# Storing and loading the bfloat16 parts of q and k one by one

## The reference

```python
def _L0_xattn_ref(query, key, value, Wq, bq, Wk, bk, Wv, bv, Wo, bo):
    q = proj(query, Wq, bq)          # B, H=16, S=256, D_K=16
    k = proj(key, Wk, bk)
    v = proj(value, Wv, bv)
    q = q * cos + _rotate_half(q) * sin
    k = k * cos + _rotate_half(k) * sin
    scores = jnp.einsum('bhqd,bhkd->bhqk', q, k) / np.sqrt(D_K)
    scores = jnp.where(dist <= WINDOW, scores, -1e9)     # WINDOW = 50
    p = jax.nn.softmax(scores, axis=-1)
    out = jnp.einsum('bhqk,bhkd->bhqd', p, v)
    return out @ Wo.T + bo
x = x + jnp.tanh(g_xattn[0]) * _L0_xattn_ref(_layernorm(x), ctx_1024, ctx_1024, ...)
x = x + jnp.tanh(g_ffn[0]) * _L0_ffn_ref(_layernorm(x), L0_ffn_w_gate, L0_ffn_w_up, L0_ffn_w_down)
```

## Time and profile before

| what | value |
|---|---|
| median of three runs | 1368.07 us (1368.03 to 1373.25) |
| the profiled execution: its own time | 1368.83 us |
| its span, first to last instruction | 1367.1 us |
| mean granted TensorE clock | 0.965 |
| TensorE busy (matmul) | 1203.8 us, 88% |
| VectorE busy | 1212.9 us, 89% |
| ScalarE busy | 826.5 us, 60% |
| GpSimd busy | 549.5 us, 40% |
| moved by DMA | 207.27 MB, mean 152 GB/s |

### The profile page before, as it was taken

How to read it: one execution, slowest core, us unless ns; L and a number is a source line. 1 busy time by engine, 2 the same in 40 slices (tenths; PEclk the granted TensorE clock), 3 DMA queues, 4 the chain that set the end, 5 groups by cost and what they waited for, 6 DMA issues and landing times. The chain is left out here.

```text
span 1367.1 us, 27802 instructions
## 1 busy us (share of the span) xinstructions
PE 1203.8 (88%) x8963; PEld 786.5 (58%) x8995; DVE 1212.9 (89%) x3603; ACT 826.5 (60%) x1336; POOL 549.5 (40%) x1357
## 2 busy tenths in 40 slices
PE   5689898989998988998988659998999799968998
PEld 3457666666666666666666434443433334427887
DVE  3799999999999999999998849997999989988886
ACT  2255656666666665656565536665677599983332
POOL 1177777777777777777776610000000000000000
PEclk9699999999999999999999869999999999988999
DMA  2757575757565666666664202223455455546764
GB/s 78 156 121 183 135 174 139 168 139 164 143 161 146 158 151 153 154 151 158 146 161 112 102 8 93 111 97 127 158 183 185 159 191 196 199 165 205 241 225 169
DMA packets 132369, 207.27 MB, mean 152 GB/s; under 512 B 11159, under 2 KB 97050, under 8 KB 126106
## 3 DMA queue, kind: packets, MB, share of 16 engines
q1 hardware_dynamic: 132250, 205.86, 54.4%
HBM read 125.60 MB, written 79.69 MB: 150 GB/s over the span
## 5 line engine op out<-in xcount | busy, mean ns | idle before, releaser
L670 DVE CUSTOM_DVE_ANT_0 psum<-psum,band 128x178 f32<-128x178 f32 x1024 | 316.5, 372 | 38.4 <-PE psum L878 38.1
L552 ACT ACTIVATE probs<-psum 128x356 f32<-128x356 f32 x512 | 210.6, 468 | 162.7 <-PE psum L895 162.2
L486 POOL TENSOR_SCALAR_AFFINE_SELECT probs<-probs 128x154 f32<-128x154 f32 (+1 forms) x512 | 221.4, 443 | 156.5 <-ACT probs L552 150.5
L1088 PE MATMUL psum<-xnT,w_upT 128*128 (+1 forms) x1152 | 261.1, 384 | 19.0 <-DVE maxima L1312 8.8
L1088 PEld LDWEIGHTS psum<-xnT,w_upT 128*128 128x128 f16 x1152 | 109.9, 99 | 170.0 <-issue 32.6
L878 PE MATMUL psum<-k_stack,q_stack 96*128 96x178 bf16 x1024 | 141.3, 245 | 51.3 <-DVE smax L670 47.4
L495 POOL TENSOR_SCALAR_AFFINE_SELECT probs<-probs 128x254 f32<-128x254 f32 (+1 forms) x512 | 180.3, 375 | 0.0
L895 PE MATMUL psum<-q_stack,k_stack 98*128 98x178 bf16 x1024 | 136.2, 242 | 16.8 <-DMA q_stack<-shiftT 10.5
L670 DVE DVE_READ_ACCUMULATOR2_ANT smax<- 128x1 f32 x1024 | 142.9, 140 | 0.0
L1688 PE MATMUL psum<-w_downT,xnT 128*128 128x256 f16 x1152 | 128.3, 275 | 16.0 <-DVE xnT L1638 16.0
L878 PEld LDWEIGHTS psum<-k_stack,q_stack 96*128 96x128 bf16 x1024 | 74.2, 98 | 109.0 <-DVE smax L670 87.2
(11 more groups left out here) (189 smaller groups left out, 2265.3 us busy)
## 6 DMA issues: line engine op xcount, KB each, us to landing
k_parts_scratch<-k_parts SPq DMA_DIRECT2D x32, 384.0 KB, 2.5
q_parts_scratch<-q_parts SPq DMA_DIRECT2D x32, 384.0 KB, 2.6
k_stack<-k_parts_scratch SPq DMA_DIRECT2D x32, 384.0 KB, 5.1
q_stack<-q_parts_scratch SPq DMA_DIRECT2D x32, 384.0 KB, 7.3
gate_scratch<-g_stage SPq DMA_DIRECT2D x16, 768.0 KB, 3.2
g_in<-gate_scratch SPq DMA_DIRECT2D x16, 768.0 KB, 4.6
sig_scratch<-w_gateT SPq DMA_DIRECT2D x32, 384.0 KB, 2.3
sig_again<-sig_scratch SPq DMA_DIRECT2D x32, 384.0 KB, 3.4
```

The costliest lines, as they stand in the source:

```text
L486: nc.gpsimd.affine_select(out=t[:, :, 0:n], in_=t[:, :, 0:n], pattern=[[0, 2], [1, n]], compare_op=ALU.is_ge, fill=0.0, base=WINDOW - off, ...
L552: nc.scalar.activation(ring_tile(probs, b, pair, c)[:].rearrange("p e j -> p (e j)"), scoreT_bank[c][:, 0:2 * SPAN], ACT.Exp, scale=DK ** ...
L670: ins = nc.vector.tensor_tensor_reduce(out=mine, in0=mine, in1=keep["band"][:, t, :], scale=1.0, scalar=-3e38, op0=ALU.add, op1=ALU.max, a ...
L1088: last = nc.tensor.matmul(bank[:], weights[wp][:, c * I + f * P:c * I + (f + 1) * P], x_parts[:, c, bass.ds(j * (2 * TILE) + xp * TILE, TI ...
```

## The change

Each part gets its own store, of 128 KB, and is loaded as soon as the stores it waits for have landed. For k, a part goes to all row blocks that hold it, with one DMA each: three for the high part, two for the middle one, one for the low one, each of 16 rows of 8 KB (128 KB) that lie 3, 2 or 1 partitions apart. For q, a part is one DMA, as before: 384, 256 and 128 KB. So a batch has 6 stores and 9 loads where it had 2 and 6. Two semaphores per tensor take the place of one: `high_stored` for part 0, `rest_stored` for parts 1 and 2 together. The loads of parts 1 and 2 wait until both are stored. ScalarE's `high` waits for both semaphores. The store of k's high part stands ahead of the second half of b2's shift rows.

```diff
-            def store_parts(b, n):
+            def store_part(b, n, part):
                 if not b.real:
                     return
-                reached(sp, mid_ready[n], b, 1, 1)
-                reached(sp, low_ready[n], b, 1, 1)
+                reached(sp, part_ready[n][part], b, 1, 1)
                 if b.n >= NBUF:
-                    sp.wait_ge(stack_loaded[n][b.buf], b.rnd * 48)
-                sp.dma_start(scratch[n][b.buf].rearrange("k (a d) (h t) -> (d h) (k a) t", a=2, h=H),
-                             parts[n][:].rearrange("p k (a t) -> p (k a) t", a=2)).then_inc(parts_stored[n], 16)
+                    sp.wait_ge(stack_loaded[n][b.buf], b.rnd * LOADED[n])
+                sp.dma_start(scratch[n][b.buf, part].rearrange("(a d) (h t) -> (d h) a t", a=2, h=H),
+                             parts[n][:, part, :].rearrange("p (a t) -> p a t", a=2)).then_inc((rest_stored if part else high_stored)[n], 16)
-            def load_stacks(b, n):
+            def load_part(b, n, part):
...
-                reached(sp, parts_stored[n], b, 16, 16)
-                reached(sp, scoredT, b.before(NBUF), 2 * PAIRS, 2 * PAIRS)
+                if part:
+                    reached(sp, rest_stored[n], b, 32, 32)
+                else:
+                    reached(sp, high_stored[n], b, 16, 16)
+                    reached(sp, scoredT, b.before(NBUF), 2 * PAIRS, 2 * PAIRS)
                 row = 0
                 for g in range(3):
                     rows = (3 - g) * DK
-                    sp.dma_start(stack[row:row + rows, :, :].rearrange("r s t -> r (s t)"), scratch[n + "_rows"](b.buf, g)).then_inc(stack_loaded[n][b.buf], 16)
+                    if n == "q" and g == part:
+                        sp.dma_start(stack[row:row + rows, :, :].rearrange("r s t -> r (s t)"),
+                                     scratch[n][b.buf, part].unsqueeze(1).to_broadcast([DK, 3 - g, H * S]))\
+                            .then_inc(stack_loaded[n][b.buf], 16)
+                    if n == "k" and part < 3 - g:
+                        sp.dma_start(stack[row + part:row + rows:3 - g, :, :].rearrange("r s t -> r (s t)"),
+                                     scratch[n][b.buf, part]).then_inc(stack_loaded[n][b.buf], 16)
                     row += rows
...
                 load_residual(Batch(rnd, unit, 3))
+                store_part(Batch(rnd, unit, 0), "k", 0)
                 load_shift(Batch(rnd, unit, 2), 1)
-                store_parts(Batch(rnd, unit, 0), "k")
-                store_parts(Batch(rnd, unit, 0), "q")
-                load_stacks(Batch(rnd, unit, 0), "k")
-                load_stacks(Batch(rnd, unit, 0), "q")
+                b0 = Batch(rnd, unit, 0)
+                store_part(b0, "k", 1)
+                load_part(b0, "k", 0)
+                store_part(b0, "k", 2)
+                store_part(b0, "q", 0)
+                load_part(b0, "k", 1)
+                load_part(b0, "k", 2)
+                load_part(b0, "q", 0)
+                store_part(b0, "q", 1)
+                store_part(b0, "q", 2)
+                load_part(b0, "q", 1)
+                load_part(b0, "q", 2)
                 load_shift(Batch(rnd, unit, 1), 0)
...
-                reached(act, parts_stored[n], b.before(1), 16, 16)
+                reached(act, high_stored[n], b.before(1), 16, 16)
+                reached(act, rest_stored[n], b.before(1), 32, 32)
```

More of the change, by code:

```diff
@@ L277, in attention @@
         xres_loaded = [sem(f"xres_loaded{k}") for k in range(NBUF)]
-        parts_stored = {n: sem(f"{n}_parts_stored") for n in "qk"}
+        high_stored, rest_stored = ({n: sem(f"{n}_{size}_stored") for n in "qk"} for size in ("high", "rest"))
         stack_loaded = {n: [sem(f"{n}_stack_loaded{k}") for k in range(NBUF)] for n in "qk"}
@@ L298, in attention @@
         mid_ready = {n: sem(f"{n}_mid_ready") for n in "qk"}
+        part_ready = {n: (high_ready[n], mid_ready[n], low_ready[n]) for n in "qk"}
         shiftT_copied, exp_done = sem("shiftT_copied"), sem("exp_done")
@@ L317, in attention @@
         rows_c = ctx_in.rearrange("b (t p) d -> b p t d", p=P)
+        LOADED = {"q": 16 * 3, "k": 16 * 6}
         def run(steps):
@@ L700, in round_weight @@
                 if m == 0:
-                    dve.wait_ge(parts_stored["q"], 16 * B)
+                    dve.wait_ge(high_stored["q"], 16 * B)
+                    dve.wait_ge(rest_stored["q"], 32 * B)
                 if n == "w_down":
@@ L870, in scores @@
                 if pair == 0:
-                    pe.wait_ge(stack_loaded["k"][b.buf], b.rnd * 48 + 48)
-                    pe.wait_ge(stack_loaded["q"][b.buf], b.rnd * 48 + 48)
+                    pe.wait_ge(stack_loaded["k"][b.buf], (b.rnd + 1) * LOADED["k"])
+                    pe.wait_ge(stack_loaded["q"][b.buf], (b.rnd + 1) * LOADED["q"])
                 for t in range(T):
@@ L1707, in build @@
     for n in "qk":
[L1709 to L1718, removed]
+        scratch[n] = nc.dram_tensor(f"{n}_parts_scratch", (NBUF, 3, DK, H * S), BF16, kind="Internal").ap()
     with ExitStack() as ctx:
```

## The result

The changed kernel takes 1383.28 us in the median of five runs (1378.52 to 1385.75). The kernel before, run beside it, takes 1369.82. The ratio is 1.0089, 95% interval [1.0059, 1.0118]: slower by 0.9%, outside the range I gave (1358 to 1378) and on the side of the second rival.

What follows compares the result with a forecast made beforehand. VectorE and TensorE together were taken to pace the batches. Gains of 0.5 (steady part), 1.1 (last unit) and 0.5 us (first batch) summed to 2.1, giving 1366.0 us on the median, range 1358 to 1378.

Steps and rivals of the forecast that it cites:

- second rival: SyncE's two new waits hold back the shift rows: 1411 us, or 1376 in a mild form; chance 0.12.
- What bounds the kernel: Steady batches: VectorE and TensorE together pace them at 22.48 us; transfers have about 1.1 us of room.
- The extra issuing on SyncE: SyncE's queue: issuing grows from 4.4 to 7.6 us per batch, the extra 3.2 us covered by its free time.
- wait for k's rest stores: SyncE, before loading k1 and k2: k2's store lands 2.5 us after issue, at 416.1.
- It lands at 418.9 + 2.5 + 0.8 = 422.2: q's last rest store: issued at 418.9, 2.5 us to land, 0.8 more for the q load ahead.
- The price of lateness: TensorE's shift-row waits: 1.41 us costs 0.24, 1.81 costs 0.29, anything beyond counts one to one.
- half-way case: Shift rows landing half way between forecast and second rival: TensorE waits 1.1 us and it costs nothing.
- The ends: First batch and last unit with q and k work: gains of 0.5 and 1.1 us.
- strong form (1411): Second rival with both stores landing after 4.8 us: TensorE waits 3.0 us, 1.5 us lost in each of 29 batches.
- The third: Rival: VectorE's small subtraction collides with GpSimd's addition in each batch, 30 us slower, 1398 us; chance 0.05.
- first rival: All shift-row waits go and each one counts, 17.4 us in total: 1351 us; chance 0.12.
- the profile's signs: Right: batches 22.48 us apart, shift waits under 0.9; wrong: rest-store waits over 4, shift waits over 1.8, batches 23 or more.

Runs made afterwards that it cites:

- e2: Changed kernel with q's two rest stores issued ahead of the loads of k's rest and q's high part: 1365.97 us, 0.9984 of the kernel before.
- e3: Changed kernel with only k split, q stored whole in one DMA and loaded in three: 1366.12 us, 0.9981 of the kernel before.
- e4: Changed kernel with only q split, k stored and loaded as before the change: 1393.78 us, 1.0181 of the kernel before.
- e5: Changed kernel with only the 384 KB load of q's high part moved behind q's rest stores: 1368.74 us, 0.9998 of the kernel before.
- e6: Kernel before, with SyncE requesting the first half of the shift rows only after q's stack loads landed: 1402.57 us, ratio 1.0247.
- e7: Changed kernel with q's rest stores early and the shift request ahead of the last two q loads: 1364.65 us, 0.9967 of the kernel before.
- e11: e7 plus 14 unneeded matmuls on TensorE just ahead of its wait for the shift rows: 1363.19 us, 0.9967 of the kernel before.
- e1: Changed kernel with the first shift-row request moved ahead of the last two q loads: 1372.98 us, 1.0033 of the kernel before.

## Why the prediction was wrong, point by point

**What bounds the kernel** held. Without late shift rows a batch is 22.48 or 22.51 us in all versions, whatever its transfers do, and VectorE still sits idle about 1 us in each of them. VectorE's 27.5 us of waiting were about four fifths of its idle time, not nearly all of it, which changes nothing here.

**The extra issuing on SyncE** held: three k loads in 1.76 us, a store in 0.37 to 0.5. The wait for k's rest stores came out as computed: SyncE goes on at 424.49, 8.2 us after the first store, where I had 7.8. The Trainium skill's rule to join small transfers (DMA: Bandwidth & Descriptors, Rules for kernel authors), taken as a cost per transfer, is not borne out here: e2 and e3 carry seven and five more and are faster than before. The fixed cost of about 2 us stands in the Trainium skill, DMA: Bandwidth & Descriptors, in the section on the anatomy of one DMA, for DMAs issued from GpSimd, while these are issued by SyncE. By that formula a store of 128 KB would take an estimated 2.3 us, and k's landed in 1.8 in the median of e2.

**The step that failed is "It lands at 418.9 + 2.5 + 0.8 = 422.2".** From the end of the store requests (419.3) I had SyncE wait 2.9 us for q's rest stores. It waits 3.9 in the mean, and 4.2 in the unit shown, because they land behind the q load of 384 KB, for whose remainder I had added only 0.8 us: from the second store's issue to the landing I had 3.3 us, and it took about 4.7 (427.5 to 432.27). With smaller slips before it, the shift request comes 17.2 us after the first k store (433.50 - 416.27), where I had 15.1. The rows then land 3.6 us after their request, where I had 3.7. So they are 2.0 us later than forecast and TensorE waits 1.6 us in this unit, where I had none. I had named both the place and the reason ("new stores have loads ahead of them in the queue, which they never had") and given it a small chance. The bound I put against it, that q's old store lands under 3 us with loads behind it, was a row for the other order. e2, e4 and e5 show the order deciding: 2.3 us with no q load in front, 6.3 with q's and all of k's.

**The price of lateness was a second error.** I had read it from three rows, 0.24 to 0.29 us for waits of 1.4 and 1.8, and put one to one beyond. That is right for batches at full clock (0.2 to 0.3 in the mean, and 0.74 for e6's wait of 2.25, where my price gives 0.73), but some waits of the same length are followed by a low clock and then cost 2 us. The trace of before has no such batch in its steady part, so the rows could not show it, and the low clock was no term of my sum. My half-way case, a landing 2 us later, was priced at nothing; it cost 9.3 us in the middle, 7.8 of them in four batches with a low clock.

**The ends** were wrong by the same term. I had the first batch 0.5 us sooner; it came 1.7 later, its first scores behind a wait of 7.89 us instead of 2.96. Behind the last batch I had 1.1 us of gain and got 2.6 of loss:

```profile
758.35 0.43 PEld L917 LDWEIGHTS psum<-q_stack,k_stack 98*128 98x128 bf16 x4 [6.42 <-DMA q_stack<-shiftT]
```

**The rivals.** The first was false: with all steady shift waits gone (e2, e7) no batch is shorter. The second was right in mechanism; its strong form (1411) wasn't reached, since the waits were 1.3 us in the mean of the 23 listed (30.3 / 23) and not 3.0. I had given it 0.12. The third did not happen more often than before. The range's lower end was also slightly off its own reason: half of the first rival is 1359, not 1358.

**Of the profile's signs** that I had named, the waits for the rest stores of around 4 us and the shift waits over 1.8 are there, with batches of over 23 us only where the clock fell and at 427.

## What to carry to other kernels

When a transfer is cut into parts to start sooner, look at what each part will find in front of it in the DMA queue and at who stands behind the wait for its landing. Here the place of two 128 KB stores, before or after one load, decided between a gain of 0.2% and a loss of 0.9%, and what came too late were two transfers of 4 KB each that the change didn't touch. A late transfer also has two prices: the lateness beyond the room there is, and, where it idles TensorE, now and then a stretch at half clock that here cost more than the lateness (by estimate 1.3 us against 0.9 in e6).

## What the runs showed of the hardware

- TensorE waits of 1.6 to 2.3 us in the steady part were sometimes followed by some 3 us at a granted clock of 0.50 and sometimes not: of two waits in e6, the one of 2.02 us was, the one of 2.25 was not. What decides it stays open. Filling 0.94 us of the wait with matmuls that nobody needs cut the falls from 13 to 3 of 26.
- With k's loads split the DMA engines were less busy at the same rate: 66% from 100 to 700 us at 155 GB/s before, 59% at 154 GB/s with k alone split (e3), 56% at 154 GB/s with both (e7). Why was not tried.
- Every trace, that of before included, has one batch, between 424 and 451 us, where VectorE's tiny subtraction takes 1.27 us, against a median of 0.27 (436.44 in the changed kernel). I had made a rival of it; it comes once per execution. In all 13 traces GpSimd's addition of 1.26 us had begun 0.01 to 0.03 us before it; a batch later, in the kernel before, it began 0.05 us after the subtraction, which then took 0.18. That the two get in each other's way is argued from this and was not tried.
- The clock can fall in that batch too, with no wait for shift rows: behind the slow subtraction TensorE waits 1.16 us for VectorE's maxima, in the kernel before and in e7 alike. The clock stayed at 1.00 before (23.39 us for the batch) and in e11 (23.40), and fell in e1, e2, e3, e5 and e7 (24.76 to 25.80 us).
